# Quantising the hidden layer on GpSimd and summing squares on ScalarE in an SSM block with a ternary feed-forward

## What is computed

```python
def _quant_act(x):
    scale = 127.0 / clip(max(abs(x), axis=-1), EPS)
    return clip(round(x * scale), -128, 127) / scale
x = x + ssm(_layernorm(x), W_in, W_out, ...)       # h = h*Abar + u*Bbar along time
h = gelu(_bitlinear(_layernorm(x), w1))            # _bitlinear: quantised x, ternary w
x = x + _bitlinear(h, w2)
```

## Time and profile before

| | us |
|---|---|
| median of 3 runs | 2281.41 (2273.93 to 2288.75) |
| the profiled execution | 2285.0 |
| span of its slowest core (core 2), first to last instruction | 2283.4 |
| spans of the eight cores | 2263.8 to 2283.4 |

### The profile page before, as it was taken

How to read it: one execution, slowest core, us unless ns; L and a number is a source line. 1 busy time by engine, 2 the same in 40 slices (tenths; PEclk the granted TensorE clock), 3 DMA queues, 4 the chain that set the end, 5 groups by cost and what they waited for, 6 DMA issues and landing times.

```text
span 2283.4 us, 34173 instructions; the slowest of 8 cores (2263.8 to 2283.4 us)
## 1 busy us (share of the span) xinstructions
PE 1290.4 (57%) x12248; PEld 903.5 (40%) x12248; DVE 1490.0 (65%) x2187; ACT 444.0 (19%) x682; POOL 222.9 (10%) x175
## 2 busy tenths in 40 slices
PE   0002222211111126788878778887887888788797
PEld 0001121111111115456545645654564565456564
DVE  3555555555555557777777777777777777777643
ACT  0002222211110113222212222221222222122210
POOL 0000000011111111001001100100110010001000
PEclk9999999999999998889889888988988888888888
DMA  4784444111111100001000000100000010000000
GB/s 138 258 238 126 132 138 157 41 43 46 46 46 46 46 19 20 19 20 38 20 20 29 29 20 19 39 20 19 29 29 20 20 38 20 20 20 29 10 20 19
DMA packets 33900, 120.18 MB, mean 53 GB/s; under 512 B 4996, under 2 KB 4996, under 8 KB 33732
## 3 DMA queue, kind: packets, MB, share of 16 engines
q1 hardware_dynamic: 16740, 56.11, 7.7%
q0 software_dynamic: 10656, 38.80, 4.9%
q10 hardware_dynamic: 6336, 23.07, 3.3%
HBM read 101.19 MB, written 16.78 MB: 52 GB/s over the span
## 4 chain that ended last, share of the span: by engine, by line
DVE 43%; PE 27%; DMA 10%; issue 9%; ACT 5%; DVEq 4%; POOLq 2%; ACTq 1%; SPq 0%; POOL 0%
PE pout L789 13%; DVE hred L599 10%; DMA vs<-w 4%; PE pm1a L733 3%; DVE TLblk L539 3%; DVE vs L533 3%; ACT xnfm L324 3%; DMA h_sb<-w 2%; PE pmisc L763 2%; DMA out_s<-w 2%; DVE xn L556 2%; PE pm1b L733 2%; POOLq L207 2%; PE pT L753 2%; DVE TLblk L553 2%
## 5 line engine op out<-in xcount | busy, mean ns | idle before, releaser
L789 PE MATMUL pout<-t2T,k 128*128 128x512 bf16 x2048 | 523.1, 420 | 4.1 <-DVEq L504 4.1
L789 PEld LDWEIGHTS pout<-t2T,k 128*128 128x128 bf16 x2048 | 214.8, 107 | 290.3 <-issue 112.3
L733 PE MATMUL pm1b<-k1fm,t1T 128*128 128x128 bf16 x4096 | 289.3, 237 | 63.3 <-ACTq L305 63.3
L733 PEld LDWEIGHTS pm1b<-k1fm,t1T 128*128 128x128 bf16 x4096 | 271.7, 107 | 67.7 <-issue 67.7
L733 PE MATMUL pm1a<-k1fm,t1T 128*128 128x128 bf16 x4096 | 263.0, 225 | 0.0
L622 DVE TENSOR_TENSOR vs<-h_sb,sc2bc 128x1024 f32<-128x1024 f32 x128 | 156.8, 1225 | 146.8 <-ACTq L334 75.1
L599 DVE TENSOR_REDUCE hred<-h_sb 128x128 f32<-128x4096 f32 x32 | 227.0, 7093 | 32.4 <-ACTq L305 26.6
L733 PEld LDWEIGHTS pm1a<-k1fm,t1T 128*128 128x128 bf16 x4096 | 245.6, 101 | 3.6 <-issue 1.0
L753 PE MATMUL pT<-identb,xn 128*128 128x128 bf16 x512 | 54.2, 270 | 297.1 <-DVEq L558 297.1
L694 PE MATMUL pT<-identb,k 128*128 128x128 bf16 x512 | 64.8, 306 | 189.2 <-DVEq L476 189.2
L753 PEld LDWEIGHTS pT<-identb,xn 128*128 128x128 bf16 x512 | 43.2, 121 | 312.4 <-issue 307.2
(11 more groups left out here) (152 smaller groups left out, 1341.0 us busy)
## 6 DMA issues: line engine op xcount, KB each, us to landing
vs<-w ACTq DMA_DIRECT2D x44, 512.0 KB, 4.9
h_sb<-w SPq DMA_DIRECT2D x42, 512.0 KB, 4.4
xb<-xh SPq DMA_DIRECT2D x32, 512.0 KB, 3.5
xb<-xo SPq DMA_DIRECT2D x32, 512.0 KB, 3.5
out<-out_s POOLq DMA_DIRECT2D x32, 512.0 KB, 3.0
h_sb<-w POOLq DMA_DIRECT2D x21, 512.0 KB, 5.2
out_s<-w POOLq DMA_DIRECT2D x21, 512.0 KB, 5.4
xn<-win SPq DMA_DIRECT2D x1, 256.0 KB
```

What stands on the lines that cost most here:

```text
L733: ti = t.matmul(reg, t1T[:, k * 4096 + m * 128:k * 4096 + (m + 1) * 128], k1fm[oi % 2][:, k * 128:(k + 1) * 128], start=(k == 0), stop=(k ...
L789: ti = t.matmul(pout[:, d * 512:(d + 1) * 512], k2[:, hk * 128:(hk + 1) * 128], t2T[:, hk * 1024 + d * 512:hk * 1024 + d * 512 + 512], sta ...
```

## The change

The DVE reductions over the squares go to ACT: a new `se_copy2` and `se_copy1` each pass `scr_sq` through an ACT copy with an accumulated sum; the copy's own output goes into `xn`, where it is overwritten before use. `r2d` and `r1d` now come from ACT, and DVE waits for them. ACT's list is set anew: `se_copy2(b+1)` stands behind gelu group 3, `se_copy1(b+2)` behind group 4, both square roots behind group 5. In stage 1, `se_copy1(b+2)` stands between the copy `xnfm` of chunk b+1 and the square root.

K2 goes from DVE to POOL (`gp_k2`), at the end of POOL's step, behind the output DMA. It works in `scr_sq`, and signals each quarter by `k2q`. mm2 starts its first half after two quarters and the second half after four; gelu waits for the quarter of h that it writes over, not for the whole of K2.

```diff
+            def gp_k2(oi):
+                for q in range(4):
+                    if q == 0:
+                        g.wait_ge(S["bce"], oi + 1)
+                        g.wait_ge(S["k1s_"], min(oi + 3, NCH))
+                        g.wait_ge(S["r1d"], min(oi + NCH + 4, NIT))
+                        g.wait_ge(S["r2d"], min(oi + 3, NCH))
+                    if oi >= 1:
+                        g.wait_ge(S["m2h"], 4 * (oi - 1) + q + 1)
...
+                    g.tensor_tensor(sj, hs, bcb, ALU.mult)
+                    g.drain()
+                    g.tensor_scalar(k2[:, q * 1024:(q + 1) * 1024], scr_sq[:],
+                                    TL["C_t"][:, 0:1], TL["nC_t"][:, 0:1],
+                                    op0=ALU.add, op1=ALU.add)
+                    g.drain().then_inc(S["k2q"], 1)
...
+                if 0 <= oi1 < NCH:
+                    gp_k2(oi1)
...
-                if g == 0 and oi >= 1:
-                    s.wait_ge(S["k2_"], oi)
+                if oi >= 1:
+                    s.wait_ge(S["k2q"], 4 * (oi - 1) + g // 2 + 1)
+                    if g == 0:
+                        s.wait_ge(S["hmax"], oi)
...
+            def se_copy2(it):
+                oi = it - NCH
+                s.wait_ge(S["sq2a"], oi + 1)
+                s.wait_ge(S["xnT"], it + 1)
+                s.activation(xn[:], scr_sq[:], AF.Copy, bias=0.0, scale=1.0,
+                             accum_out=TL["sq2u"][:, 0:1])
+                s.drain().then_inc(S["r2d"], 1)
+
+            def se_copy1(it):
+                s.wait_ge(S["sq1a"], it + 1)
+                if it >= 1:
+                    s.wait_ge(S["xnT"], it)
+                s.activation(xn[:], scr_sq[:], AF.Copy, bias=0.0, scale=1.0,
+                             accum_out=TL["sq"][:, 0:1])
+                s.drain().then_inc(S["r1d"], 1)
...
-                    for g in range(0, 5):
+                    for g in range(0, 4):
                         se_gelu(oi1, g)
+                if NCH <= b + 1 < NIT:
+                    se_copy2(b + 1)
+                if has1:
+                    se_gelu(oi1, 4)
+                if b + 2 < NIT:
+                    se_copy1(b + 2)
+                if has1:
+                    se_gelu(oi1, 5)
                 if NCH <= b + 1 < NIT:
                     se_sqrt2(b + 1)
                 if b + 2 < NIT:
                     se_sqrt1(b + 2)
...
-                v.wait_ge(S["sq2a"], oi + 1)
-                v.tensor_reduce(TL["sq2u"][:, 0:1], scr_sq[:], AX.X, ALU.add)
-                D_().then_inc(S["r2d"], 1)
+                v.wait_ge(S["r2d"], oi + 1)
...
-                v.wait_ge(S["sq1a"], it + 1)
-                v.tensor_reduce(TL["sq"][:, 0:1], scr_sq[:], AX.X, ALU.add)
-                D_().then_inc(S["r1d"], 1)
+                v.wait_ge(S["r1d"], it + 1)
...
-                v.wait_ge(S["bce"], oi + 1)
-                for q in range(4):
-                    if oi >= 1:
-                        v.wait_ge(S["m2h"], 4 * (oi - 1) + q + 1)
...
-                D_().then_inc(S["k2_"], 1)
...
-                    t.wait_ge(S["k2_"], oi + 1)
+                    t.wait_ge(S["k2q"], 4 * oi + 2)
...
+                else:
+                    t.wait_ge(S["k2q"], 4 * oi + 4)
```

More of the change, by code:

```diff
@@ L137, in build_nc @@
             "k1s_", "k1T", "k1fm_", "mm1", "gelu", "hmax", "hmaxT", "sc2_",
-            "rowT", "rowe", "bcmm", "bce", "k2_", "m2h", "outv", "od", "pTe"]
+            "rowT", "rowe", "bcmm", "bce", "k2q", "m2h", "outv", "od", "pTe"]
     with ExitStack() as ctx:
@@ L217, in gp_sq1 @@
                 g.drain().then_inc(S["sq1a"], 1)
+            def gp_k2(oi):
[7 more added lines that the diff above has]
+                        g.wait_ge(S["m2h"], 4 * (oi - 1) + q + 1)
+                    hs = h_sb[:, q * 1024:(q + 1) * 1024].rearrange(
+                        "p (m t) -> p m t", m=8)
+                    sj = scr_sq.rearrange("p (m t) -> p m t", m=8)
+                    bcb = sc2bc.unsqueeze(1).broadcast_to([128, 8, 128])
+                    g.tensor_tensor(sj, hs, bcb, ALU.mult)
[4 more added lines that the diff above has]
+                    g.drain().then_inc(S["k2q"], 1)
             gp_sq1(0)
@@ L221, in _ @@
             for b in range(NIT + 3):
+                oi1 = b - NCH - 1
                 oi3 = b - NCH - 3
@@ L334, in se_rowbc @@
                 s.drain().then_inc(S["bce"], 1)
+            se_copy1(0)
             se_sqrt1(0)
+            se_copy1(1)
             se_sqrt1(1)
@@ L353, in _ @@
                 if has1:
-                    for g in range(5, 8):
-                        se_gelu(oi1, g)
+                    se_gelu(oi1, 6)
+                    se_gelu(oi1, 7)
                 if 0 <= b - NCH < NCH:
```

## The result

The changed kernel takes 2536.5 us, the kernel before 2280.8 us (10 runs each); the ratio is 1.111, 95% interval 1.1085 to 1.114. It is slower by 256 us; 2296 us had been forecast, 15 more than before. Its profiled core has a span of 2534.6 us, 251.2 more than before. Taken apart at the starts of `u_s` (DVE's first instruction of a step): stage 1, from the first `u_s` to the 32nd, fell from 353.8 to 281.7 us (-72); stage 2, from the 32nd to the last, rose from 1350.0 to 1649.0 us (+299); what follows the last `u_s` rose from 142.6 to 160.0 us (+17); the start of stage 1 lies 7 us later, which is no effect of the change: it lies between 424 and 444 us on the changed kernel's eight cores, and between 430 and 441 on those of before.

The account below looks back on a forecast made before the run. No engine is full; each step is a loop of waits. From 2285.0 us, -76 for stage 1 and +92 for stage 2 give 2301, or 2296 after adjusting to the median and last step; range 2264 to 2350.

Parts of the forecast that it names:

- K2 on POOL: Stage 2, POOL's queue: a quarter takes 4.0 us, K2 16 us, ending 4.6 behind the next step's start, delaying hardly anything.
- the 6.9 up to which it is covered: Stage 2: K2 may end up to 6.9 us behind the step's start without delay, allowing a one-input pass of 2.5.
- L205 waits for K2: Stage 2, POOL: the square of x2 waiting for K2 would show the forecast wrong; no size given.
- rival (1): POOL's queue: K2 becomes the bound ahead of the next step's squares, about 2450 us, or 2356 at 3.0; chance 0.13.
- Stage 1: Scan-to-scan loop: sum of squares leaves DVE, norm precedes Pool's square; period 9.06 us, gain 2.53 per step, -76 in sum.
- The ACT sums in stage 2: Stage 2, ACT's list: the sum waits behind gelu group 3, so DVE goes on later; loss 2.55 us per step.
- rival (3): ACT: the sums need extra table loads, 1.28 us each, up to four per step; +150, about 2440 us; chance 0.05.
- The scan held by K2: Stage 2, DVE: the scan may wait 0 to 1.89 us for the running POOL instruction; 0.5 per step taken.
- K2 leaving DVE gains nothing: Stage 2: K2's 8.2 us of DVE per step lie in PE's shadow; L592 still waits 0.48 us for PE.

Follow-up runs that it names:

- e1: Changed kernel with K2 back on DVE, the sums still on ACT: 2289.5 us, 1.006 of the kernel before.
- e4: Changed kernel with POOL's rounding pass of K2 left out, the product going straight to bf16: 2279.3 us, 1.002 of the kernel before.
- e5: Not labelled in the text; apparently the changed kernel with POOL's rounding pass given immediates (2513 us) or cut to one operation (2400 us).
- e10: Changed kernel with one quarter of K2 on DVE and three on POOL: 2368.8 us, 1.039 of the kernel before.
- e6: Changed kernel with K2 on DVE and the sums on ACT in stage 1 only: 2207.9 us, 0.969 of the kernel before.
- e2: Changed kernel with the sums back on DVE in ACT's earlier order, K2 still on POOL: 2602.5 us, 1.142 of the kernel before.
- e9: Kernel before with POOL's square of x replaced by a one-input maximum pass: 10.78 us per stage 1 step, near 44.4 in stage 2; total not given.
- e7: K2 and the sum over x2's squares on DVE, sum over x's squares on ACT, roots earlier in stage 2: 2213.9 us, 0.973 of the kernel before.
- e8: K2 on DVE, ACT sums in stage 1 only, DVE's stage 2 sum of x moved under POOL's square: 2182.8 us, 0.959 of the kernel before.

## Why the prediction was wrong

**K2 on POOL: the step that failed.** The text bounded the one-input pass between 0.81 and 3.78 us and took 1.89, the square's row, "one input less than the 1.89 product". It is 3.78, the upper bound; the product itself is 2.35, not 1.89 (its inputs are two tensors, one of them spread by a broadcast, and the square's one; which of the two costs the 0.46 was not tested). A quarter is 6.5 us instead of 4.0, K2 26.1 instead of 16, and its end lies 15.0 us behind `u_s`, beyond the 6.9 up to which it is covered. That excess of 8.1 us enters every full step; `e1`, `e4`, `e5` and `e10` show it together with its threshold, and L205 waits for K2, one of the signs of being wrong that the text named. So rival (1) came about, with its mechanism, place and threshold as written, and was given 0.13. Its price was too low as well, 153 us, where taking K2 off POOL again (`e1`) gives back 247: it kept 1.89 for the product and 0.2 for the gaps (0.43 measured), and counted nothing for the last steps (+17). Both of its prices, 2356 and 2450, lay above the 2350 at which the stated range ended.

The reason for the low chance was not in any row: that fewer inputs mean less time. On VectorE such a pass is the shorter one, 0.81 against 1.23. On POOL it is the longer one, 2.77 us with one operation and 3.63 with two. With nothing measured for a new instruction on an engine, the terms should have been carried through the threshold from both ends: 16 us of K2 per step at 1.89 left 2.3 us of room, four passes of 0.6 us more. All prices from 2.5 us up to the bound of 3.78 lay on the wrong side.

The Trainium skill (GPSIMD Engine Reference, section on engine selection) calls one-input work on GpSimd roughly line-rate, from which the prediction had estimated about 1 us. The runs here show 2.77 us for one operation on 128x1024 float32 and 3.63 to 3.78 for two; the measurement decides. For the two-input product the same page's figure (section on elementwise cycle accounting), 4497 ns at 2048 elements, gives an estimate of 2.25 us at half the size, and 2.35 was measured.

**Stage 1: right.** Forecast 9.06 us per step from 11.59, measured 9.19 on average and 9.05 in most steps. Both parts came: the sum on ACT is covered, and the norm at 3.92 behind the scan precedes Pool's square, so L600 is 0.16. -76 forecast, -72 measured.

**The ACT sums in stage 2: right, though hidden by K2.** 2.55 us per step forecast; `e1` less `e6` gives 47.27 - 44.44 = 2.83, with DVE's two places met to 0.05 us. The pass is 1.06 us and 0.19 for the accumulator, 1.25 as taken. The other 0.3 lies in mm2's second part (9.46 us on average against 9.17). No table load was added, the trace has 63 before and after: rival (3) is out. The loss shows where K2 ends within its cover (`e1`, `e4`); in the changed kernel it isn't there (`e2`).

**The scan held by K2: 0.5 forecast, nothing measured, and that by its place.** In the changed kernel 29 scans fall under POOL's one-input pass, 0.93 to 3.22 us behind its start [for one, the last three rows of the stage 2 timeline]. 28 take their usual 0.47 to 0.48 us, and the one at 0.93 takes 0.52. In `e10` the scan also comes earlier under the same pass:

```profile
1460.86 3.78 POOL L236 TENSOR_SCALAR k<-xn,TLblk 128x1024 bf16<-128x1024 f32 x1 [0.18 <-issue]
1461.13 1.18 DVE L542 TENSOR_TENSOR_SCAN h_s<-abt,h_s,u_s 64x128 f32<-64x128 f32 x1 [0.19 <-issue]
```

On its eight cores 65 scans began 0.23 to 0.97 us behind the pass's start, and all ended 1.46 us behind it; the 167 later ones took 0.48. So the scan can be held, as the prediction had it, but by the one-input pass for about its first 1 us only, as L525 and L553 were in `e9`. The Trainium skill (SBUF — State Buffer, section on who interferes with whom) has the lock held for the whole instruction; with POOL's square of x the trace agrees (L574 1.70 us under it), with its one-input pass it doesn't.

**K2 leaving DVE gains nothing: right.** With K2 back on DVE (`e1`) and with its product on POOL (`e4`) the step is 47.3 and 47.4 us.

**What stays open.** How the granted clock in mm2's second part depends on what went before: where K2 ends within its cover, its mean length was between 8.8 us (`e7`) and 9.8 (`e9`) against 9.1 before, and this moved steps by up to 0.6 us without a clear rule. What in POOL's one-input pass takes the time was measured, not explained.

## What to carry to other kernels

Idle time of an engine is no reason to move work to it: ask what stands behind that work in the engine's own list, and up to which duration it is covered. Where the new instruction has no row, work out the duration at which the cover ends and spend a measurement on that one instruction before all else. A wait put down to one engine can be another's fault: follow the releaser's own row one step further before the order of lists is changed.

## What the runs showed of the hardware

- POOL's pass with one tensor input, 128x1024 float32: 2.77 us with one operation and an immediate, bf16 or float32 out, 3.63 with two, 3.78 with two per-partition scalars. Its products: 1.89 us for x times x, 2.35 for two tensors, one of them broadcast.
- A 128x1 DVE product with two SBUF inputs that starts under a POOL square ends with it, within 0.02 us (0.56 us in `e8` to 1.72 in the kernel before, where 0.16 is its length alone). If it starts early under a POOL one-input pass it ends 1.04 us behind the pass's start (`e9`), and a scan that started in the pass's first 0.97 us 1.46 behind it (`e10`).
- DVE's one-input rounding pass into bf16 took 2.67 us under POOL's product of K2 (`e10`), 0.81 without it (`e1`). Its one-input sum with an accumulator was not held by POOL's square (1.22 us, `e8`), and its instructions with one input in PSUM and one in SBUF not by POOL's product: 0.69 us for `x2`'s halves, in 28 steps in which one was running.
- It works the other way too: POOL's product that began under DVE's took 3.20 us instead of 2.35 (`e10`).
- An ACT copy of 128x1024 float32 with a sum: 1.06 us, and 0.19 for reading the accumulator.
